# Second attention of an audio tower: minus mu as three rows of the score product, and the middle parts of q and k rounded on Pool

## What is computed

```python
x = layernorm(h, eps 1e-5), then layernorm again with eps 1e-6, gamma, beta
q, k, v = split_heads(x @ Wq.T + bq), ...          # 16 heads of 16 columns
scores = einsum('bhqd,bhkd->bhqk', q, k) / 4
scores = sigmoid(scores - mu) * exp(scores)
scores = scores / sum(scores, axis=-1)
out = einsum('bhqk,bhkd->bhqd', scores, v), joined, @ Wo.T + bo;  h = h + out
```

## Time and profile before

| | |
|---|---|
| median of 3 runs | 779.44 us (777.09 to 789.72) |
| span of the profiled execution | 779.1 us |
| MoE stage, about | 245 to 535 us |
| second attention, about | 535 to 738 us |
| TensorE busy | 707.4 us (91%) |
| VectorE busy | 442.6 us (57%) |
| ScalarE busy | 357.8 us (46%) |
| GpSimd busy | 129.2 us (17%) |
| mean granted TensorE clock | 0.955 of full speed |

### The profile page before, as it was taken

One profiled execution on the slowest core, in us unless ns is written; L12 is line 12 of the kernel. 1 busy time (PEld: TensorE's weight loads), 2 busy tenths in 40 slices (PEclk: granted clock), 3 DMA queues, 4 the chain that ended last, 5 costly groups with the idle time before them and its releaser, 6 DMA issues.

```text
span 779.1 us, 16167 instructions
## 1 busy us (share of the span) xinstructions
PE 707.4 (91%) x5688; PEld 580.0 (74%) x5696; DVE 442.6 (57%) x1125; ACT 357.8 (46%) x610; POOL 129.2 (17%) x166
## 2 busy tenths in 40 slices
PE   5687999999989999999999999998899999998635
PEld 4466878878768999999999999996566665665423
DVE  3557688888673342344222232332788898866666
ACT  3242454345533212122212112213998989988435
POOL 2010122232132210000001001002634222210000
PEclk9699999999999999999999999999999999999855
DMA  6979166355737566555555555571875447651002
GB/s 172 213 133 262 31 97 102 79 86 87 121 109 268 189 209 223 189 192 172 180 189 181 199 192 177 169 180 46 101 113 95 67 63 104 82 65 18 1 14 95
DMA packets 70839, 102.54 MB, mean 132 GB/s; under 512 B 8416, under 2 KB 58600, under 8 KB 70640
## 3 DMA queue, kind: packets, MB, share of 16 engines
q1 hardware_dynamic: 67376, 93.15, 50.7%
q0 software_dynamic: 3136, 8.40, 4.2%
q10 hardware_dynamic: 256, 0.07, 0.0%
HBM read 63.75 MB, written 12.58 MB: 98 GB/s over the span
## 4 chain that ended last, share of the span: by engine, by line
PE 61%; DVE 17%; ACT 7%; DMA 7%; issue 5%; POOL 1%; SPq 1%; ACTq 1%; DVEq 0%; POOLq 0%
PE psum L1981 18%; PE psum L2032 17%; DVE arena L1304 9%; DMA arena<-arena 5%; PE psum L1661 4%; PE psum L1924 3%; PE psum L1685 2%; PE psum L1930 2%; ACT arena L830 2%; PE psum L1939 1%; POOL w0T L699 1%; PE psum L2009 1%; DVE arena L1157 1%; PE psum L2149 1%; PE psum L1654 1%
## 5 line engine op out<-in xcount | busy, mean ns | idle before, releaser
L1981 PEld LDWEIGHTS psum<-arena 128*128 128x128 f32 x1248 | 144.9, 192 | 2.1 <-issue 0.3
L1981 PE MATMUL psum<-arena 128*128 128x128 f32 x1248 | 146.1, 275 | 0.1
L2032 PE MATMUL psum<-arena 128*128 x624 | 141.4, 380 | 0.8 <-DVE arena L1450 0.8
L859 ACT ACTIVATE arena<-psum,arena 128x128 f32<-128x128 f32 x156 | 44.5, 368 | 194.7 <-PE psum L1981 115.2
L2032 PEld LDWEIGHTS psum<-arena 128*128 128x128 f32 x624 | 115.5, 190 | 15.4 <-issue 1.2
L1432 DVE TENSOR_SCALAR arena<-psum,arena 128x128 f32<-128x128 f32 x156 | 44.0, 345 | 80.5 <-PE psum L1981 67.3
L1939 PE MATMUL psum<-arena 96*128 96x256 bf16 x512 | 75.1, 274 | 9.1 <-ACT arena L829 5.7
L1304 DVE TENSOR_TENSOR arena<-arena 128x1024 f32<-128x1024 f32 x64 | 79.9, 1316 | 4.5 <-ACT arena L829 2.6
L1939 PEld LDWEIGHTS psum<-arena 96*128 96x128 bf16 x512 | 44.3, 97 | 44.0 <-ACT arena L829 14.4
L699 POOL DMA_INDIRECT w0T<-yg,pos x32 | 37.4, 1169 | 222.6 <-DMA yg<-arena 176.2
L1450 DVE TENSOR_TENSOR arena<-psum,arena 128x256 f32<-128x256 f32 x39 | 16.6, 425 | 96.6 <-PE psum L2032 96.6
(11 more groups left out here) (290 smaller groups left out, 1207.8 us busy)
## 6 DMA issues: line engine op xcount, KB each, us to landing
arena<-in_L_ffn_w_dram SPq DMA_DIRECT2D x47, 1024.0 KB, 5.1
arena<-arena SPq DMA_DIRECT2D x192, 128.0 KB, 5.1
arena<-xg SPq DMA_DIRECT2D x39, 128.0 KB, 2.0
yg<-arena SPq DMA_DIRECT2D x39, 128.0 KB, 1.7
out_dram<-arena SPq DMA_DIRECT2D x8, 256.0 KB, 2.1
xg<-zeros SPq DMA_DIRECT2D x9, 128.0 KB, 2.9
arena<-in_x_dram SPq DMA_DIRECT2D x8, 128.0 KB, 3.1
arena<-in_L_ffn_b_dram SPq DMA_DIRECT2D x1, 1024.0 KB, 14.9
```

Of the source, the lines that this page charges most:

```text
L859: ins = act.activation(hidT[:, v, c, :], psum[:, 2 * v, c * P:(c + 1) * P], ACT.Relu, bias=b1c[:, v, c:c + 1])
L1981: mm = pe.matmul(psum[:, 2 * v + c // HALF, (c % HALF) * P:(c % HALF + 1) * P], w1b[:, i % W1_BUFS, d, c * P:(c + 1) * P], xtT[:, v, d, :] ...
L2032: mm = pe.matmul(y_bank, hidT[:, u, c, :], w2s[:, one(e), c, :].rearrange("p o n -> p (o n)"), start=(c == 0), stop=(c == HC - 1))
```

## The change

Three things are edited, all for the second attention.

1. **Minus mu in the product.** The Sigmoid activation loses its bias operand. Instead the Sigmoid pass's scores contract 99 rows (`MU_ROWS`), three more than before: in the stacks of q these rows hold ones, in the stacks of k three bf16 parts of -mu. Sigmoid belongs to the second pass for even batches and to the first for odd ones, and `scores` gets its number of rows accordingly.
2. **Preparation of these rows.** VectorE makes the parts of -mu at MoE tile 7 (`mu_parts`, seven small chained instructions). Pool fills rows 96 to 127 of stack 0 of q with ones and of k with the parts, ahead of its first gather, when the first layer of the tenth tile is done. SP copies the three rows into the stacks 1, ahead of batch 1's spreads, after waits for the end of the MoE stage. TensorE waits for the rows ahead of batch 0's and batch 1's first scores.
3. **The middle parts of q and k on Pool.** For batches 1 to 7 `second_part` moves from ScalarE to Pool, behind the addition of bo; `scale1(b+2, 0)` moves ahead of `gather(b+3)`. Batch 0's `second_part` stays on ScalarE, in the MoE tiles.

```diff
+MU_PARTS = 3
+MU_ROWS = ROWS + MU_PARTS
...
+                def mu_rows_copied():
+                    sp.wait_ge(S["l2_mm"], MOE_TILES)
+                    sp.wait_ge(S["y_ev"], MOE_TILES)
+                    for u in range(2):
+                        sp.wait_ge(y_st[u], 16 * ((MOE_TILES + 1 - u) // 2))
+                    sp.wait_ge(S["consts"], ROW_CONSTS + 2)
+                    for stack in (stackq1, stackk1):
+                        sp.dma_start(stack[1][ROWS:MU_ROWS], stack[0][ROWS:MU_ROWS]).then_inc(S["w_in"], 16)
+
                 def iteration(b, u, k):
+                    if b == 0:
+                        mu_rows_copied()
...
+                def second_part(b, which, got, done):
+                    pool.wait_ge(got, b + 1)
+                    pool.tensor_copy(n_qkp[which][:, 1], n_qkr[which]).then_inc(done, 1)
...
+                    if stages(b + 1, 1, LAST):
+                        second_part(b + 1, 0, S["n_qr"], S["n_qm"])
+                        second_part(b + 1, 1, S["n_kr"], S["n_km"])
+                    if stages(b + 2, 0, LAST):
+                        scale1(b + 2, 0, S["n_mv"], S["n_eps"], S["n_rstd"])
                     if stages(b + 3, 4, LAST):
                         gather(b + 3)
-                    if stages(b + 2, 0, LAST):
-                        scale1(b + 2, 0, S["n_mv"], S["n_eps"], S["n_rstd"])
...
+                pool.wait_ge(S["l1_hi"], EARLY_TILES + 2)
+                pool.memset(stackq1[0][ROWS:P], 1.0).then_inc(S["consts"], 1)
+                pool.wait_ge(S["consts"], ROW_CONSTS + 1)
+                pool.wait_ge(S["p_const"], MU_STEPS)
+                pool.tensor_scalar(stackk1[0][ROWS:P], stackq1[0][ROWS:P], mu_r[ROWS:P, 2:3], None, ALU.mult
+                                   ).then_inc(S["consts"], 1)
...
-                    return act.activation(out, in_, ACT.Sigmoid, bias=neg_mu[:])
+                    return act.activation(out, in_, ACT.Sigmoid)
...
-                    if stages(b + 1, 0, LAST):
-                        second_part(b + 1, 0, S["n_qr"], S["n_qm"])
                     pass1(5)
-                    if stages(b + 1, 0, LAST):
-                        second_part(b + 1, 1, S["n_kr"], S["n_km"])
                     pass1(6)
...
+                    if i == 7:
+                        mu_parts()
...
-                                           stackk1[u][0:ROWS, hd, kt * P:(kt + 1) * P], stackq1[u][0:ROWS, hd, :],
+                                           stackk1[u][0:rows, hd, kt * P:(kt + 1) * P], stackq1[u][0:rows, hd, :],
...
-                            scores(b, u, p, S["s1_mm"])
+                            scores(b, u, p, S["s1_mm"], (ROWS, MU_ROWS)[u])
...
-                            scores(b, u, p, S["s2_mm"])
+                            scores(b, u, p, S["s2_mm"], (ROWS, MU_ROWS)[v])
```

More of the change, by code:

```diff
@@ L124, in tower_kernel @@
         neg_mu = sb("neg_mu", [P, 1], F32)
+        mu_p = sb("mu_p", [P, 2], BF16)
+        mu_r = sb("mu_r", [P, 3], F32)
         ones_row = sb("ones_row", [1, P], F32)
@@ L399, in tower_kernel @@
         WT_STEPS = 10
+        CONST_STEPS = 7
+        MU_STEPS = CONST_STEPS + 7
+        ROW_CONSTS = 15
         PLAN_STEPS = 22
@@ L717, in iteration @@
                         scale1(b - 1, 1, S["m_mv"], S["m_eps"], S["m_rstd"])
+                pool.wait_ge(S["l1_hi"], EARLY_TILES + 2)
[4 more added lines that the diff above has]
+                                   ).then_inc(S["consts"], 1)
+                pool.wait_ge(S["consts"], ROW_CONSTS + 2)
                 for b in range(2):
@@ L1420, in weight_rounded, with mu_link, mu_parts @@
                     assert steps[0] == W8_STEPS
+                mu_steps = [CONST_STEPS]
+                def mu_link(ins):
+                    mu_steps[0] += 1
+                    ins.then_inc(S["p_const"], 1)
+                    dve.wait_ge(S["p_const"], mu_steps[0])
+                def mu_parts():
+                    dve.wait_ge(S["wT_done"], WT_STEPS + 3)
+                    mu_link(dve.tensor_copy(mu_p[:, 0:1], neg_mu[:]))
+                    mu_link(dve.tensor_tensor(mu_r[:, 0:1], neg_mu[:], mu_p[:, 0:1], ALU.subtract))
+                    mu_link(dve.tensor_copy(mu_p[:, 1:2], mu_r[:, 0:1]))
+                    mu_link(dve.tensor_tensor(mu_r[:, 1:2], mu_r[:, 0:1], mu_p[:, 1:2], ALU.subtract))
+                    mu_link(dve.tensor_tensor(mu_r[:, 2:3], mu_p[:, 0:1], ident[:, ROWS:ROWS + 1], ALU.mult))
+                    mu_link(dve.scalar_tensor_tensor(out=mu_r[:, 2:3], in0=mu_p[:, 1:2], scalar=ident[:, ROWS + 1:ROWS + 2],
+                                                     in1=mu_r[:, 2:3], op0=ALU.mult, op1=ALU.add))
+                    mu_link(dve.scalar_tensor_tensor(out=mu_r[:, 2:3], in0=mu_r[:, 1:2], scalar=ident[:, ROWS + 2:ROWS + 3],
+                                                     in1=mu_r[:, 2:3], op0=ALU.mult, op1=ALU.add))
+                    assert mu_steps[0] == MU_STEPS
                 def tile(i, u):
@@ L1932, in project_token_tile, with scores @@
                     return mm
-                def scores(b, u, p, done):
+                def scores(b, u, p, done, rows):
                     for i in range(2):
@@ L2065, in pass1 @@
                                 pe.wait_ge(S["set_done"], 3)
+                                pe.wait_ge(S["consts"], ROW_CONSTS + 2)
+                            if b == 1 and p == 0:
+                                pe.wait_ge(S["w_in"], LATE_LOADS + 2 * 16)
                             if p == 0:
```

## The result

The changed kernel takes 790.21 us (median of 14 runs, 787.04 to 795.49); the kernel before, in the same measurement, 785.24 us (median of 14, 777.09 to 789.72). The medians lie 5.0 us apart; the ratio over all runs is 1.0088 with a 95% interval of 1.0064 to 1.0113, so some 7 us slower. Measured once more (6 runs) it was 1.0125, 1.0074 to 1.0175. The forecast was 777.4 us in a range of 774.8 to 783.0: the measured time lies above the range, and the change has the other sign. Its size stays within the 2% that the chances went by.

A forecast was written before the change was run, and what follows sets the result against it. In the second attention no engine is full, so the order of waits decides. Sigmoid bias -0.63, batch 0's k copy +0.27 and freed multiplies -1.6 make -2.0 us: 777.4 us against the 779.44 median, range 774.8 to 783.0.

The forecast's parts named there:

- the cover of Pool's memset and product: MoE stage: Pool's 176.2 us of idle time hides the two instructions that prepare the -mu rows; cost 0.
- The add of bo leaves the multiplies: Second attention, four batches: moved gathers push Pool's add behind VectorE's multiplies, freeing 1.07 us each; -1.6 us in all.
- Pool gets in at every multiply: Rival, second attention: Pool's scale1 and add stretch multiplies, +0.93 us in four batches; 782.8 us, chance 0.13.
- the 0.4 that I let TensorE pass on: Second attention: of 1.07 us leaving a batch's multiplies, 0.4 us shortens the batch, in four batches.
- The bias: Second attention: Sigmoid without its column operand saves 89 ns on one activation a batch on the path; -0.63 us.
- The casts worth nothing: Second attention: removing ScalarE's two casts a batch gains nothing, since its eighth first-pass activation waits for TensorE's scores anyway.
- The three rows: Second attention, Sigmoid scores: contracting 99 rows instead of 96 costs 0, under 0.4 us in all either way.
- Pool's copies: Second attention: two 128x512 copies a batch on Pool take 0.75 us each; up to 1.2 us is hidden.
- the +0.27: Batch 0 of the second attention: Pool's copy locked out by VectorE delays the last part of k, +0.27 us once.
- The late gathers: Second attention, batches 4 to 7: gathers issued behind scale1(b+2) still deliver before combine wants their data; hidden, no cost.
- only the bias counts: Rival, second attention: what the add gives back is lost at normalise or to TensorE; 779.1 us, chance 0.25 including no gain.

The follow-up runs named there:

- the four kernels: Changed kernel with Pool's product replaced by a memset, split in two, split in sixteen, or made on VectorE: ratios 1.0003, 0.9975, 0.9983, 1.0001 to the kernel before.

## Why the prediction was wrong

**The step that failed: the cover of Pool's memset and product.** "Pool idles 176.2 us in that stage ... this covers the links ... and the two Pool instructions." Pool's idle time covers Pool's time; it says nothing of VectorE, whose copy Pool's instruction held up to its end. I asked whether Pool was free, and not who would be locked out. Instead of 0 it cost 6.7 and 8.0 us in the two profiles, and put the time above the kernel before. The earlier trace rows held the pattern with the roles exchanged, and the prediction quoted the rule for VectorE instructions with two SBUF inputs, for the second attention alone. The Trainium skill, SBUF — State Buffer, section "Who interferes with whom", says of copies as well that they can run in a mode that takes the shared ports, and that who issues first keeps them for the whole instruction while the other stops; the 8.60 us agree, and so do the 0.68 us of the reduce beside it, which it says never contends on this chip. I had priced neither a Pool instruction of 10 us nor who issues behind it.

**The add of bo leaves the multiplies: -1.6, measured 0.** A pattern and a size failed here. Pool was not shut out behind the fourth gather: L705, L707 and L731 each got in at the next multiply. The six microseconds of the earlier trace rows did come again in batch 0 (the gather at 569.78 takes 5.68), but they don't carry over to the steady batches. One sign of the forecast came true all the same, by luck: the second multiply takes 1.22 us in batches 1 to 4 and 2.30 in batch 5, because the stretch had moved to the fourth or fifth multiply, and not away. So the rival "Pool gets in at every multiply" had the mechanism; its price was wrong too, since scale1's two small instructions stretched no multiply (1.22 us each) and only the add did, by the same 1.07. And the 0.4 that I let TensorE pass on is 0.62 when the add is really gone.

**What was right.** The bias: 1034 ns for 1122, and a pitch of 24.49 to 24.50 for 24.58 in five batches, 0.4 us in all (0.63 forecast). The casts worth nothing, with TensorE as the releaser of the eighth activation. The three rows: eight matmuls of scores take 1.04 us with 99 rows, as with 96. Pool's copies: 0.61 us for 0.75, and 1.01 in batch 0, where one was to be locked out; but the +0.27 put on that doesn't show (24.98 from batch 0 to 1, where it was 25.05). The late gathers: hidden. Without the stall, the four kernels lie at 0.9990, near the 0.9996 of the rival "only the bias counts" (779.1 against 779.44); the times hardly part that from the forecast's 0.9974, the pitches do.

**The base.** 5.8 of the 12.8 us between forecast and result are the difference between 779.44, the median of three runs that I had, and 785.24, that of 14. The three ranged over 12.6 us, which the range of 8 us ignored.

## What to carry to other kernels

An instruction that is put on an idle GpSimd is not free because GpSimd is idle: look for the VectorE instructions that will issue while it runs, copies of a few columns too, and count the slack of what waits for them. If the work is needed, cut it into short instructions, or give it to VectorE, which did it here in 1.28 us instead of 10.64. And before a change of less than 1% is forecast, look at how far the runs of the kernel itself lie apart.

## What the runs showed of the hardware that I had not expected

- A copy of 8 elements per partition on VectorE took 8.60 us instead of 0.17 and ended with a GpSimd product; beside a memset on GpSimd, which reads nothing, the same copy took 1.42 us and ended with the memset.
- VectorE's instructions with a PSUM operand (0.42 us) and its reduce from SBUF (0.68 us) ran beside the same product at the times that they have in the kernel before.
- The product of 32 x 4096 bf16 by a column took 10.64 us on GpSimd, 16.0 in sixteen pieces, and 1.28 on VectorE.
- A stop of TensorE was paid twice here: behind 4.86 us of idle time the next 32 matmuls took 5.44 us in one execution and 6.75 in another, instead of 3.73, and behind 2.10 us of idle time the granted clock was 0.50.
